# Local attention: softmax's inverse row sums multiplied into the probabilities on POOL, ahead of their transposes

## The reference, cut to what matters

```python
        def _layer(x, wqkv, qs, ksc, wo, lg, lb, w1, b1, w2, b2):   # x: 2 x 2048 tokens x 256
            h = shift_token(x)
            q, k, v = jnp.split(h @ wqkv, 3, axis=-1)              # 8 heads of 64
            ...
            q = l2norm(q) * qs
            k = l2norm(k) * ksc
            q, k = rotary_xpos(q, k)
            o = local_attention(q, k, v)
            x = x + o.reshape(b, n, INNER) @ wo
            ...

        # local_attention: windows of 128 queries, keys of this window and of the one before
            sim = jnp.einsum('bhwid,bhwjd->bhwij', bq * 8.0, bk)
            sim = jnp.where(mask, -jnp.finfo(sim.dtype).max, sim)
            attn = jax.nn.softmax(sim, axis=-1)
            out = jnp.einsum('bhwij,bhwjd->bhwid', attn, bv)
```

## Time and profile before

| what | value |
| --- | --- |
| median of 3 runs | 2222.87 us (2220.17 to 2224.51) |
| the profiled execution | 2226.4 us, its span 2224.6 us |
| mean granted TensorE clock | 0.959 of full speed |
| PE busy | 2018.6 us (91%) |
| DVE busy | 1587.9 us (71%) |
| ACT busy | 1090.7 us (49%) |
| POOL busy | 454.4 us (20%) |
| first and last product L845 | 824.2 and 1953.6 us |

### The profile page before, as it was taken

How to read it: one execution, slowest core, us unless ns; L and a number is a source line. 1 busy time by engine, 2 the same in 40 slices (tenths; PEclk the granted TensorE clock), 3 DMA queues, 4 the chain that set the end, 5 groups by cost and what they waited for, 6 DMA issues and landing times. The chain is left out here.

```text
span 2224.6 us, 43241 instructions
## 1 busy us (share of the span) xinstructions
PE 2018.6 (91%) x13920; PEld 1719.0 (77%) x13920; DVE 1587.9 (71%) x4601; ACT 1090.7 (49%) x2533; POOL 454.4 (20%) x273
## 2 busy tenths in 40 slices
PE   6799999999999959999999689995999999959998
PEld 6688878878878847888888577774888888858887
DVE  5547636636636668889999477775899999946777
ACT  3332222232222228888888433332777777733333
POOL 0100000000000014444444111111444444410111
PEclk9899999999999979999999799997999999969999
DMA  7200000000000020000000100001000000000010
GB/s 252 52 1 1 1 1 1 1 2 1 1 2 1 1 101 6 5 5 5 6 5 5 52 10 10 10 5 63 5 5 6 5 5 5 5 19 10 10 57 28
DMA packets 42351, 42.51 MB, mean 19 GB/s; under 512 B 8497, under 2 KB 36870, under 8 KB 42249
## 3 DMA queue, kind: packets, MB, share of 16 engines
q1 hardware_dynamic: 40114, 35.90, 5.0%
q10 hardware_dynamic: 2134, 5.26, 0.6%
HBM read 32.76 MB, written 8.39 MB: 18 GB/s over the span
## 5 line engine op out<-in xcount | busy, mean ns | idle before, releaser
L887 ACT ACTIVATE l_probs<-l_probs,l_negmax 128x256 f32<-128x256 f32 x512 | 253.1, 496 | 64.6 <-DVE l_negmax L968 64.6
L115 PE MATMUL ps<-local_w_hi,l_xT 128*128 128x512 f32 x384 | 167.4, 436 | 36.1 <-DVE l_xT L961 30.1
L841 POOL TENSOR_TENSOR l_t<-l_t,l_t 128x1024 f32<-128x1024 f32 x64 | 152.9, 2389 | 196.3 <-DVE l_t L1014 196.3
L845 POOL TENSOR_TENSOR l_t<-l_t,l_rnorm 128x1024 f32<-128x1024 f32 x64 | 122.0, 1906 | 306.7 <-DVE l_rnorm L985 306.7
L115 PE MATMUL ps<-attn_w_hi,attn_xT_hi 128*128 128x512 f32 x392 | 168.6, 430 | 12.3 <-issue 9.7
L392 ACT ACTIVATE attn_exp<-ps 128x512 f32<-128x512 f32 x130 | 77.7, 599 | 205.7 <-PE ps L117 205.7
L893 ACT ACTIVATE l_probsT<-ps 128x512 f32<-128x512 f32 x256 | 138.7, 594 | 55.0 <-PE ps L1112 55.0
L116 PE MATMUL ps<-attn_w_lo,attn_xT_hi 128*128 128x512 f32 x392 | 158.3, 404 | 0.0
L117 PE MATMUL ps<-attn_w_hi,attn_xT_lo 128*128 128x512 f32 x392 | 158.2, 404 | 0.0
L117 PE MATMUL ps<-local_w_hi,l_xT 128*128 128x512 f32 x384 | 155.1, 404 | 0.0
L116 PE MATMUL ps<-local_w_lo,l_xT 128*128 128x512 f32 x384 | 154.9, 403 | 0.0
(11 more groups left out here) (202 smaller groups left out, 5916.0 us busy)
## 6 DMA issues: line engine op xcount, KB each, us to landing
tok_x<-x SPq DMA_DIRECT2D x16, 512.0 KB, 4.4
m_shifted<-shifted SPq DMA_DIRECT2D x18, 256.0 KB, 2.7
shifted<-x SPq DMA_DIRECT2D x64, 64.0 KB, 1.5
out<-x SPq DMA_DIRECT2D x8, 512.0 KB, 3.7
ffn_w_raw<-ffn_w SPq DMA_DIRECT2D x6, 640.0 KB
local_w_raw<-ffn_wqkv SPq DMA_DIRECT2D x4, 768.0 KB, 5.2
h<-txt SPq DMA_DIRECT2D x4, 512.0 KB, 4.9
attn_w_raw<-attn_Wq ACTq DMA_DIRECT2D x1, 1024.0 KB, 7.0
```

The source lines that it names most:

```text
L115: nc.tensor.matmul(out, wh, mh, start=start, stop=False, skip_group_check=True)
L841: nc.gpsimd.tensor_tensor(t1[:], t1[:], t2[:], ALU.add).then_inc(s.summed.sem, 1)
L845: nc.gpsimd.tensor_tensor(r, r, rn[:].unsqueeze(2).to_broadcast([P, 2 * LH, DH]), ALU.mult).then_inc(s.rotated.sem, 1)
L887: last = nc.scalar.activation(v, v, ACT.Exp, bias=nb[:, h:h + 1], scale=-1.0, accum_out=rsum[:, h:h + 1])
```

## The change

POOL no longer spreads the inverse row sums. When DVE has them, it multiplies each pair's probabilities in place by their heads' inverses (`normalise`, four products of 128x512 per tile), and PE's transposes of the probabilities wait for these (`scaled`) where they waited for the exponentials. The four transposes of the inverses, ACT's copy of them and DVE's product with them are gone; ACT and DVE read the output's high and low parts from PSUM. Together with that:

- on PE, the output projection goes ahead of pairs 0 and 1, and the V projection goes between pairs 0, 1 and pairs 2, 3; the x transposes stand directly behind pair 3;
- on DVE, all eleven operations of the inverse norm stand behind heads 2 to 7, two behind each head and the last behind head 7; the x edge stands behind head 1;
- the clamp is a maximum over two slots, of which one holds 1e-24;
- the even window's mask is made by POOL.

```diff
@@ POOL
-            def spread_out(t):
+            def normalise(t, r):
-                wait(pool, s.r_t, t)
                 pool.wait_ge(*s.inverted.after(t + 1))
-                wide = rinv[:].unsqueeze(2).to_broadcast([P, LH, DH])
-                nc.gpsimd.tensor_tensor(spread[:].rearrange("p (h d) -> p h d", d=DH), wide,
-                                        one[:].unsqueeze(2).to_broadcast([P, LH, DH]), ALU.mult).then_inc(s.spread.sem, 1)
+                for pair in range(LPAIRS):
+                    v = pm[:, pair].rearrange("p (e k) -> p e k", e=2)
+                    nc.gpsimd.tensor_tensor(v, v, rinv[:, 2 * pair:2 * pair + 2].unsqueeze(2).to_broadcast([P, 2, 2 * P]),
+                                            ALU.mult).then_inc(s.scaled.sem, 1)
...
+            def even_mask(t):
+                wait(pool, s.masked, 4 * (t - 1))
+                nc.gpsimd.tensor_tensor(mask_e[:, P:2 * P], prev[:], negs[:, bass.ds(t // 2, 1)].to_broadcast([P, P]),
+                                        ALU.add).then_inc(s.mask_set.sem, 1)
...
                 if late:
-                    spread_out(t - 2)
+                    normalise(t - 2, r)
+                if r == 1:
+                    even_mask(t - 1)
@@ ACT
                 if d:
-                    wait(act, s.o_norm, n - 2)
-                    wait(act, s.y_full, n - 3)
-                    nc.scalar.activation(oth[:], on[:], ACT.Copy).then_inc(s.o_hi.sem, 1)
+                    wait(act, s.o_full, n - 2)
+                    nc.scalar.activation(oth[:], ps[:, OT], ACT.Copy).then_inc(s.o_hi.sem, 1)
...
-                if c:
-                    wait(act, s.r_t, n - 1)
-                    wait(act, s.o_done, n - 2)
-                    nc.scalar.activation(on[:], ps[:, RB], ACT.Copy).then_inc(s.r_out.sem, 1)
@@ DVE
                 if k == 0:
-                    return nc.vector.tensor_scalar(ss[:], ss[:], 1e-24, None, ALU.max)
+                    return nc.vector.tensor_reduce(ssc[:], ss[:], AX.X, ALU.max)
...
-                if b and r == 1:
-                    chain(nc.vector.tensor_scalar(mask_e[:, P:2 * P], prev[:], negs[:, bass.ds((n - 1) // 2, 1)], None,
-                                                  ALU.add))
...
-                    nc.vector.tensor_tensor(otl[:], on[:], f32(oth[:]), ALU.subtract).then_inc(s.o_done.sem, 1)
+                    nc.vector.tensor_tensor(otl[:], ps[:, OT], f32(oth[:]), ALU.subtract).then_inc(s.o_done.sem, 1)
...
-                    wait(dve, s.sq_summed, n + 1)
-                    chain(rnorm(0))
-                    wait(dve, s.rotated, n)
-                    chain(rnorm(1))
-                    chain.mark(rnorm(2))
                     x_lo(n + 1, 1 - r)
+                k = 0
                 for h in range(LH):
...
                         score(n - 1, h, mask)
-                    if a:
-                        chain.wait()
-                        if 3 + h < LAST:
-                            chain.mark(rnorm(3 + h))
-                        else:
-                            rnorm(LAST).then_inc(s.rnorm.sem, 1)
-                if c:
-                    wait(dve, s.o_full, n - 1)
-                    wait(dve, s.r_out, n - 1)
-                    nc.vector.tensor_tensor(on[:], ps[:, OT], on[:], ALU.mult).then_inc(s.o_norm.sem, 1)
+                    if a and h == 1:
+                        x_edge(n + 1, 1 - r)
+                    if a and h >= 2:
+                        for _ in range(2):
+                            if k == 0:
+                                wait(dve, s.sq_summed, n + 1)
+                            if k == 1:
+                                wait(dve, s.rotated, n)
+                            if k:
+                                chain.wait()
+                            if k < LAST:
+                                chain.mark(rnorm(k))
+                            elif k == LAST:
+                                rnorm(LAST).then_inc(s.rnorm.sem, 1)
+                                break
+                            k += 1
@@ PE
             def probs_t(t, pair):
-                wait(pe, s.exped, 4 * t + pair + 1)
+                wait(pe, s.scaled, 4 * t + pair + 1)
...
-            def inverses():
-                for pair in range(LPAIRS):
-                    last = nc.tensor.transpose(ps[:, RB, pair * P:(pair + 1) * P],
-                                               spread[:, pair * P:(pair + 1) * P],
-                                               K.ident[:])
-                last.then_inc(s.r_t.sem, 1)
```

More of the change, by code:

```diff
@@ L752, in local_phase @@
     HF = DH // 2
-    (idle, one, xc, xt, sq, t1, t2, qt, kt, vv, pm, pt, on, spread, oth, otl, cos, sin, mask_e, mask_o, prev, flags, negs, qks,
-     ss, rn, tmp, nb, rsum, rinv, mean, rs, nmr, tmp32, dev), _ = mem.place(
+    (idle, xc, xt, sq, t1, t2, qt, kt, vv, pm, pt, oth, otl, cos, sin, mask_e, mask_o, prev, flags, negs, qks,
+     ss, ssc, rn, tmp, nb, rsum, rinv, mean, rs, nmr, tmp32, dev), _ = mem.place(
         K.mlp_end, mem.end,
-        (f"l{layer}_idle", [P, 1], F32), (f"l{layer}_one", [P, 1], F32), (f"l{layer}_x", [P, 2, D], F32),
+        (f"l{layer}_idle", [P, 1], F32), (f"l{layer}_x", [P, 2, D], F32),
         (f"l{layer}_xT", [P, 2, 2, 2 * XW], F32R), (f"l{layer}_sq", [P, 2, LINNER], F32),
@@ L822, in _ @@
             nc.gpsimd.memset(K.w_raw[:, KC * W1C + HC * D:FW], 0.0).then_inc(s.padded.sem, 1)
-            nc.gpsimd.memset(one[:], 1.0)
+            nc.gpsimd.memset(ss[:], 1e-24)
             nc.gpsimd.memset(kt[:, 1], 0.0)
@@ L846, in window @@
                                         ALU.mult).then_inc(s.rotated.sem, 1)
+            pool.wait_ge(*s.const_in.after(160))
             for t in range(4):
-                window(t, t >= 2)
+                window(t, t % 2, t >= 2)
             with pool.Fori(2, T // 2) as p:
-                window(2 * p)
+                window(2 * p, 0)
                 pool.wait_ge(*s.ffn_hi.after(p - 1))
@@ L990, in step @@
                 mask = mask_o if r == 0 else mask_e
-                if b and r == 1:
-                    chain(nc.vector.tensor_scalar(mask_e[:, P:2 * P], prev[:], negs[:, bass.ds((n - 1) // 2, 1)], None,
-                                                  ALU.add))
                 if c:
                     wait(dve, s.exped, 4 * (n - 1))
-                    wait(dve, s.spread, n - 2)
+                    wait(dve, s.scaled, 4 * (n - 2))
                     nc.vector.reciprocal(rinv[:], rsum[:]).then_inc(s.inverted.sem, 1)
@@ L1022, in step @@
                 if a:
[L1023 removed]
+                    nc.vector.tensor_reduce(ss[:, :, 0], sq[:].rearrange("p a (h d) -> p (a h) d", d=DH), AX.X,
                                             ALU.add).then_inc(s.sq_summed.sem, 1)
[L1025 to L1029 removed]
                     x_lo(n + 1, 1 - r)
+                k = 0
                 for h in range(LH):
                     if b:
+                        if h == 0 and r == 1:
+                            wait(dve, s.mask_set, (n + 1) // 2)
                         if h % 4 == 0:
@@ L1151, in step @@
                         last.then_inc(s.qk_t.sem, 1)
-                if c:
-                    probs_t(n - 2, 0)
-                    wait(pe, s.r_out, n - 2)
-                    probs_t(n - 2, 1)
                 if d:
@@ L1163, in step @@
                 if c:
+                    probs_t(n - 2, 0)
+                    wait(pe, s.p_done, 4 * (n - 2))
+                    probs_t(n - 2, 1)
+                if b:
+                    wait(pe, s.v_done, n - 1)
+                    project(1 - r, 2, V).then_inc(s.v_full.sem, 1)
+                if c:
                     for pair in (2, 3):
@@ L1166, in step @@
                         probs_t(n - 2, pair)
-                if b:
-                    wait(pe, s.v_done, n - 1)
-                    project(1 - r, 2, V).then_inc(s.v_full.sem, 1)
                 if a:
@@ L1173, in step @@
                     x_t(n + 1, 1 - r)
-                if c:
-                    wait(pe, s.spread, n - 1)
-                    wait(pe, s.p_done, 4 * (n - 1))
-                    inverses()
                 if b:
@@ L1185, in step @@
                     wait(pe, s.v_done, n - 1)
+                    wait(pe, s.p_done, 4 * (n - 1))
                     wait(pe, s.y_done, n - 2)
@@ L1526, in __init__ @@
         self.p_done = count("p_done")
-        self.r_t = count("r_t")
-        self.r_out = count("r_out")
-        self.spread = count("spread")
         self.inverted = count("inverted")
+        self.scaled = count("scaled")
+        self.mask_set = count("mask_set")
         self.sq_summed = count("sq_summed")
@@ L1545, in __init__ @@
         self.y_full = count("y_full")
-        self.o_norm = count("o_norm")
 class MlpCounts:
```

20 lines of the change are left out of this document (11 added, 9 removed).

## The result

The changed kernel takes 2282.35 us (median of 4 runs, 2276.48 to 2283.72) against 2221.99 us (2220.17 to 2224.51, also 4): a ratio of 1.0266, 95% interval 1.0245 to 1.0287. The forecast was 2292 us in a range of 2250 to 2315. The profiled execution took 2282.1 us, its span is 2280.3 us, 55.7 us longer than the span before.

The account below looks back on a forecast made before the run. A closed loop through PE, DVE and POOL, 13.25 us a tile, was taken as the bound. Terms sum to +1.06 a tile and +70 us in all: 2296 us profiled, 2292 us forecast, range 2250 to 2315.

Parts of the forecast that it names:

- the late pair: PE's probability pair 1 in odd tiles, kept waiting about 0.1 us by POOL's products: +3 us in all.
- Term 1: PE ahead of the scores: the four transposes of the inverses go, -0.47 us a tile on the loop.
- Term 2: PE's x transposes must wait until ACT has copied pair 2 from bank 5: +0.57 us a tile.
- Term 3: DVE from first score to last norm operation: five extra chained small operations at 0.21 us, +0.96 us a tile.
- rival A: DVE's norm chain: a second small operation costs only an independent one's 0.09 us, giving 2255 us; chance 0.12.
- Term 4: DVE's clamp, mask and product and ACT's copy of the inverses lie off the loop: 0 each.
- Term 5: POOL's four in-place products take 1.04 us each, covered except for pair 1 in odd tiles: +3 us in all.
- Term 6: Layer ends lose a DVE product and transposes, get probability transposes behind the projection: +0.5 us a layer, within -2 and +2.
- rival B: POOL's products take 1.28 or 1.5 us each and come late, giving 2303 or 2343 us; chance 0.08.
- Rival C: PE between l_t and scores: chain under 0.47 us and copy hidden, so the kernel gets faster, 2194 us; chance 0.10.
- rival D: PE's granted clock falls from 0.99 towards 0.95 through its waits: +19 us, 2311 us; chance 0.05.

Follow-up runs that it names:

- e4: Changed kernel with four transposes of the identity put ahead of the x transposes, where the inverses' four had been: 2302.12 us, ratio 1.0347 to the kernel before.
- e3: Changed kernel with the V projection in two halves, ahead of pair 2 and between pairs 2 and 3: 2250.25 us, ratio 1.0114 to the kernel before.
- e2: Kernel before with the norm operations placed two behind each of heads 2 to 6, the last behind head 7, none ahead of the scores: 2269.99 us, ratio 1.0203.
- e5: e1 plus five small independent 128x16 DVE additions, one behind each of heads 2 to 6: 2260.72 us, ratio 1.0162 to the kernel before.
- e7: Changed kernel with each of POOL's four products covering only its pair's first head, 256 of 512 columns: 2276.52 us, ratio 1.0239 to the kernel before.
- e1: Changed kernel with the norm operations placed as before, one behind each head, three around x_lo: 2239.55 us, ratio 1.0068 to the kernel before.
- e8: Changed kernel with the edits of e1 and e3 together: 2232.64 us, ratio 1.0043 to the kernel before.

## Why the prediction was right, and where it was off

The mechanism is shown: the time is set by a loop through PE, DVE and POOL that no engine fills, and the change lengthens it by 1.12 us in a tile (13.23 to 14.35 as the mean of layer 0 from its third interval on), where the forecast had 1.06 and 0.05 more for the late pair. Term by term:

- **Term 1, the transposes (-0.47).** Too large. e4 puts them back for +0.36 in the trace, and for 18 us in time, 0.29 a tile. Part of what they took is given back by a longer wait for ACT's copy and slower x transposes (e4).
- **Term 2, the x transposes' wait (+0.57).** Right: 1.36 us from pair 2 as forecast, and e3 takes it away for 0.54 in a tile.
- **Term 3, the norm chain (+0.96).** Right in sum: 4.70 - 3.72 = +0.98. e2, which has neither a norm operation nor the x edge behind heads 0 and 1, has 4.57, so the chain without them is +0.85 where the sum's prices give 5 x 0.21 - 2 x 0.09 = +0.87. The other 0.13 is the x edge, which the sum had at the 0.09 of the norm operation whose place it takes. (The Trainium skill, "VectorE: DVE Perf Modes", section "The DRAIN you can't avoid", has it of eight copies that a semaphore costs nothing extra. As a rule this would give rival A's 2255; by e2 and e5 it doesn't hold for operations of 0.17 us.)
- **Term 4, the clamp and the DVE work (0).** Right. DVE is busy for 66% of the local stretch instead of 87%, and the loop's sum closes without it. No run tests this term by itself.
- **Term 5, POOL's products (1.04 us each, +3).** The price is right to 0.01 (4.04 for four), and halving them (e7) brings 0.3% at most.
- **Term 6, ends of layers (+1 together).** This step failed in sign and size: -3.00 and -5.55, outside its own ends of -2 and +2. About 0.8 of each is, as far as the rows tell, DVE's product that went (PE's wait ahead of the last output projection fell from 2.19 to 1.41 us), and 1.4 the last product with V at the higher clock; the rest is probably clock too, which isn't shown.

The miss of 14 us (2296 by the sum for the profiled execution, 2282.1 measured) is thus 9 us from term 6 and from what lies ahead of and between the local layers, and 6 us from the intervals: 63.45 us in 62 of them, where 69 stood. These 6 us are not the running loop's. The 58 intervals behind the second one of each layer gave 65.1 us, where the sum has some 64.5. The four first ones gave -1.64 where it has +4.0: the forecast took the loop as closed from the first tile on, while the pipeline still fills there.

Rival A is out by e5 and e2, rival B by e7. Rival C's faster case would need a hidden copy and a chain under 0.47 us; the rows show both terms in full. For rival D PE's clock would have to fall in the local stretch; it is 0.99 as before.

The prices were nearly right as single edits, but effects of edits don't add: those of e1 and e3 taken from 2282 would give 2207, and e8 stands at 2233, because each shortening uncovers something else.

## What to carry to other kernels

When all engines show idle time or one is 97% busy, follow one tile from engine to engine and add up the starts; the loop's length, not the busiest engine, says what an edit is worth, and work taken off an engine at a place outside the loop brings nothing. Count dependent small operations by the distance of their starts, and put them where the engine waits anyway: moving the same eleven operations took the kernel from 2.7% slower to 0.7% slower, and further ahead, with PE's, ACT's and POOL's order changed too, to 0.4% faster, though more of that last gain lies at the ends of the layers than in the loop. After each mended stretch look again for what was covered: a gain measured alone isn't there twice.

## What was not expected of the hardware

- A 128x16 DVE operation costs 0.21 us when it waits for the one before, and 0.07 to 0.09 when it doesn't, beside reductions that read PSUM.
- POOL's broadcast product of 128x512 in place takes 1.04 us (mean 1043 ns over 108), and all 64 groups of four took 4.04 or 4.05, with DVE busy on operations that read PSUM beside most of them. In the kernel before the spread of the same size took 1.49 in every other tile, where DVE's L1001, with two SBUF inputs, had started first (906.58 against 906.94). Where the spread started first (919.39 against 919.60) it took 1.04, and L1001 1.38 instead of 0.95. The column count scales the product: 2.33 us for four of 256 columns, 4.04 for four of 512.
- The last product with V of a layer, the same 32 matmuls, took 1.97 us at a granted clock of 1.00, and 3.34 and 3.42 at 0.57 and 0.56. What set the clock in its place is open.
